# Two relational graph passes on one core: gathers grouped by three tiles in place of five, with a ring of sixteen groups

## What is computed

```python
def _rgcn_layer(x, src, dst, edge_type, w_rel, root, bias):
    seg = dst * NUM_REL + edge_type
    xs = x[src]
    sums = jax.ops.segment_sum(xs, seg, num_segments=N * NUM_REL)
    cnt = jax.ops.segment_sum(jnp.ones(seg.shape, x.dtype), seg, num_segments=N * NUM_REL)
    mean = (sums / jnp.maximum(cnt, 1.0)[:, None]).reshape(N, NUM_REL, -1)
    return jnp.einsum('nrd,rdo->no', mean, w_rel) + x @ root + bias
...
edge_type = jnp.argmax(msg[:, NODE_EMB_DIM:-NODE_EMB_DIM], axis=1)
h = relu(_rgcn_layer(layernorm_relu(x), ..., w_rel1, root1, b1))
x = x + _rgcn_layer(h, ..., w_rel2, root2, b2)
x = x + attention(layernorm_relu(x), edge_index, W_l, W_r, att, bias)
```

## Time and profile before

| what | us |
|---|---|
| median of 3 runs | 12271.99 (12270.22 to 12287.71) |
| span of the profiled execution | 12273.4 |
| prologue, to the first gather | 195.4 |
| pass 1, first gather to first gather of pass 2 | 195.4 to 4179.0 |
| pass 2, to the first gather of the attention pass | 4179.0 to 8166.8 |
| attention pass | 8166.8 to 12273.4 |

### The profile page before, as it was taken

How to read it: one execution, slowest core, us unless ns; L and a number is a source line. 1 busy time by engine, 2 the same in 40 slices (tenths; PEclk the granted TensorE clock), 3 DMA queues, 4 the chain that set the end, 5 groups by cost and what they waited for, 6 DMA issues and landing times. The chain is left out here.

```text
span 12273.4 us, 236908 instructions
## 1 busy us (share of the span) xinstructions
PE 8873.7 (72%) x59600; PEld 8089.9 (66%) x59600; DVE 7757.1 (63%) x17430; ACT 2044.9 (17%) x5895; POOL 8995.7 (73%) x9486
## 2 busy tenths in 40 slices
PE   2666677877777766666777777766777777777776
PEld 2566667777777666666777777755666666666666
DVE  4555456666666555545777777755666666766767
ACT  1000000000000000000000000014444444444442
POOL 2777777777777577777777777757777777777776
PEclk6778889999999888888988889888989998999888
DMA  5666445555555444444555555557888888888887
GB/s 132 138 138 138 86 94 116 116 117 116 117 117 117 91 82 82 82 81 95 117 116 117 116 117 117 117 122 203 236 237 233 235 235 235 236 234 235 237 235 207
DMA packets 1439046, 1838.34 MB, mean 150 GB/s; under 512 B 371751, under 2 KB 1003264, under 8 KB 1431525
## 3 DMA queue, kind: packets, MB, share of 16 engines
q0 software_dynamic: 300000, 634.20, 28.4%
q1 hardware_dynamic: 915809, 888.29, 26.5%
q10 hardware_dynamic: 221967, 300.69, 7.9%
HBM read 1361.75 MB, written 458.67 MB: 148 GB/s over the span
## 5 line engine op out<-in xcount | busy, mean ns | idle before, releaser
L653 POOL DMA_INDIRECT p_g<-htab,p_i x6250 | 5916.2, 947 | 1972.0 <-issue 1890.3
L883 PE MATMUL p_pg<-p_g,p_oh 128*120 x33600 | 4809.8, 307 | 1792.7 <-ACTq L679 1475.7
L883 PEld LDWEIGHTS p_pg<-p_g,p_oh 128*120 128x120 f32 x33600 | 4544.3, 212 | 2026.4 <-issue 1997.2
L1257 POOL DMA_INDIRECT a_g<-xlw,a_i x3125 | 2987.2, 956 | 1036.0 <-issue 869.0
L755 DVE SCALAR_TENSOR_TENSOR p_oh<-key,qbase,p_cols 128x600 f32<-128x600 f32 x3370 | 2803.1, 832 | 13.1 <-issue 13.1
L814 DVE SCALAR_TENSOR_TENSOR p_acc<-p_acc,cont,p_pg 120x129 f32<-120x129 f32 x3360 | 1166.8, 347 | 2580.0 <-PE p_pg L883 2338.4
L670 ACT ACTIVATE p_i<-src_i 128x5 int32<-128x5 int32 x1240 | 258.2, 208 | 7566.6 <-DMA p_g<-htab,p_i 6935.0
L1730 PE MATMUL a_px<-a_g,ident 128*128 x1450 | 736.8, 594 | 840.0 <-SPq L1312 782.5
L1719 PE MATMUL a_pg<-a_v,a_into 128*128 128x132 f32 x7000 | 968.6, 288 | 62.0 <-POOL a_v L1276 23.0
L1719 PEld LDWEIGHTS a_pg<-a_v,a_into 128*128 128x128 f32 x7000 | 902.5, 202 | 73.3 <-issue 31.3
L1730 PEld LDWEIGHTS a_px<-a_g,ident 128*128 128x128 f32 x1450 | 241.4, 209 | 921.4 <-issue 920.9
(11 more groups left out here) (231 smaller groups left out, 6831.3 us busy)
## 6 DMA issues: line engine op xcount, KB each, us to landing
a_xj<-xjw ACTq DMA_DIRECT2D x725, 330.0 KB
xjw<-a_g SPq DMA_DIRECT2D x625, 330.0 KB
partial<-p_acc SPq DMA_DIRECT2D x3360, 60.5 KB
a_dst<-in_dst_dram SPq DMA_DIRECT2D x625, 320.0 KB
p_s<-partial SPq DMA_DIRECT2D x2100, 60.5 KB
p_g<-htab,p_i POOLq DMA_INDIRECT x6250
a_g<-xlw,a_i POOLq DMA_INDIRECT x3125
a_xr<-xrw ACTq DMA_DIRECT2D x728, 66.0 KB
```

Source lines behind the costliest of these rows:

```text
L653: pool.indirect_dma_start(gath[:, (k * G + q) * W:(k * G + q + 1) * W], None, table, bass.IndirectOffsetOnAxis(ap=stage[k][:, q:q + 1], ax ...
L883: last = t.matmul(pg[bank(c, k)], onehot[b][:, q * KW:(q + 1) * KW], gath[:, ds(to + q * W, W1)], start=(q == 0), stop=(q == G - 1))
L1257: pool.indirect_dma_start(gbuf[k][:, q * W:(q + 1) * W], None, xlw, bass.IndirectOffsetOnAxis(ap=stage[k][:, q:q + 1], axis=0)).then_inc(s ...
```

## The change

In the two relational passes a group is three tiles (`RG`) in place of five: 1042 groups, the last one of two tiles, and 2100 steps of three products in place of 1680 of five (210 rounds in place of 168). The ring has 16 groups (48 tiles), slots go back nine groups later in place of five, and the node tiles are read from round 106 on in place of 64. The `match` instruction covers 360 columns in place of 600. The number of gathers, of windows and of node tiles stays, and so does the attention pass with its groups of five. In the prologue the rows of one number for each group grow from 625 to 1042 where they belong to the relational passes; the group's number in the packed table gets 11 bits; the last destinations of both kinds of group are loaded.

```diff
-QSTEPS = -(-(GROUPS + NW - 1) // UN) * UN
+RG = 3
+RGROUPS = -(-TILES // RG)
+QSTEPS = -(-(RGROUPS + NW - 1) // UN) * UN
...
-READ_AT = 64
+READ_AT = 106
...
-QSLOTS = 10
-FREED = 5
+QSLOTS = 16
+FREED = 9
...
-QPACK = 1024
-PTOP = (QSLOTS - 1) * G * W * QPACK + GROUPS
+QPACK = 2048
+RW = RG * W
+PTOP = (QSLOTS - 1) * RW * QPACK + RGROUPS
...
-                            sp.dma_start(last_i, dst.rearrange("(a g e) -> a g e", a=1, e=GE)[:, :, GE - 1]).then_inc(s_last, 16)
+                            ends = dst[0:(RGROUPS - 1) * RG * P].rearrange("(a g e) -> a g e", a=1, e=RG * P)
+                            sp.dma_start(last_i[:, 0:RGROUPS - 1], ends[:, :, RG * P - 1]).then_inc(s_last, 16)
+                            sp.dma_start(last_i[:, RGROUPS - 1:], dst[E - 1:E].rearrange("(a e) -> a e", a=1)).then_inc(s_last, 16)
+                            sp.dma_start(last_a, dst.rearrange("(a g e) -> a g e", a=1, e=GE)[:, :, GE - 1]).then_inc(s_last, 16)
...
-                        nc.gpsimd.iota(gnum, [[1, GROUPS]], base=0, channel_multiplier=0, allow_small_or_imprecise_dtypes=True).then_inc(s_iota, 1)
+                        nc.gpsimd.iota(gnum, [[1, RGROUPS]], base=0, channel_multiplier=0, allow_small_or_imprecise_dtypes=True).then_inc(s_iota, 1)
...
+                        nc.gpsimd.memset(key_f[:, TILES:], -1.0).then_inc(s_iota, 1)
...
-                            dve.wait_ge(s_last, 16)
+                            dve.wait_ge(s_last, 48)
...
-                                link(v.tensor_scalar(junk, psf[:, 0:GROUPS], snum[:, c:c + 1], 0.0, how, ALU.add, accum_out=to[:, c:c + 1]))
+                                link(v.tensor_scalar(junk[:, 0:of], psf[:, 0:of], snum[:, c:c + 1], 0.0, how, ALU.add, accum_out=to[:, c:c + 1]))
...
-                            for step in ring_steps(slots, GROUPS):
+                            for step in ring_steps(slots, RGROUPS):
...
-                                counted(1, gs, QCOLS, ALU.is_lt)
+                                counted(1, gs, QCOLS, ALU.is_lt, RGROUPS)
...
-                                counted(2, lw, WCOLS, ALU.is_le)
+                                counted(2, lw, WCOLS, ALU.is_le, RGROUPS)
...
-                                counted(3, gt, SCOLS, ALU.is_lt)
+                                counted(3, gt, SCOLS, ALU.is_lt, GROUPS)
...
-                            t.matmul(psf[:, 0:512], ones[0:1, :], of[0:1, 0:512], start=True, stop=True)
-                            t.matmul(psf[:, 512:GROUPS], ones[0:1, :], of[0:1, 512:GROUPS], start=True, stop=True).then_inc(s_psf, 1)
+                            for at in range(0, width, 512):
+                                upto = min(at + 512, width)
+                                last = t.matmul(psf[:, at:upto], ones[0:1, :], of[0:1, at:upto], start=True, stop=True)
...
-                        spread(0, finq)
-                        spread(1, lastw)
-                        spread(2, fint)
+                        spread(0, finq, RGROUPS)
+                        spread(1, lastw, RGROUPS)
+                        spread(2, fint, GROUPS)
...
-                gath = sbuf(st, f"{name}_g", [P, QSLOTS * G * W])
...
-                onehot = [sbuf(st, f"{name}_oh{k}", [P, G * KW]) for k in range(QLOOK)]
+                gath = sbuf(st, f"{name}_g", [P, QSLOTS * RW])
...
+                onehot = [sbuf(st, f"{name}_oh{k}", [P, RG * KW]) for k in range(QLOOK)]
...
-                            for q in range(G):
+                            for q in range(min(RG, TILES - RG * g)):
...
-                                    gath[:, (k * G + q) * W:(k * G + q + 1) * W], None, table,
+                                    gath[:, (k * RG + q) * W:(k * RG + q + 1) * W], None, table,
...
-                        for i in range(0, GROUPS // QSLOTS):
-                            for k in range(QSLOTS):
-                                group(QSLOTS * i + k, k)
-                        for k in range(GROUPS % QSLOTS):
-                            group(GROUPS - GROUPS % QSLOTS + k, k)
+                        for g in range(RGROUPS):
+                            group(g, g % QSLOTS)
...
-                                gate(act, "act", (s_g[k], 16 * G * (i + 1)))
+                                gate(act, "act", (s_g[k], 16 * (RG * i + min(RG, TILES - RG * (QSLOTS * i + k)))))
...
-                            v.scalar_tensor_tensor(onehot[k][:, :].rearrange("p (t n) -> p t n", t=G),
-                                                   key_f[:, ds(within(gp1 * G - G, TILES - G), G)].rearrange("p (t a) -> p t a", a=1).to_broadcast([P, G, KW]),
+                            v.scalar_tensor_tensor(onehot[k][:, :].rearrange("p (t n) -> p t n", t=RG),
+                                                   key_f[:, ds(within(gp1 * RG - RG, RGROUPS * RG - RG), RG)].rearrange("p (t a) -> p t a", a=1).to_broadcast([P, RG, KW]),
...
-                                                   colsp.rearrange("p (a n) -> p a n", a=1).to_broadcast([P, G, KW]),
+                                                   colsp.rearrange("p (a n) -> p a n", a=1).to_broadcast([P, RG, KW]),
...
-                                    gp1, to = count(packed[k]), within(packed[k] >> 10, (QSLOTS - 1) * G * W)
+                                    gp1, to = count_g(packed[k]), within(packed[k] >> 11, (QSLOTS - 1) * RW)
...
-                                    for q in range(G):
+                                    for q in range(RG):
...
-                                                        start=(q == 0), stop=(q == G - 1))
+                                                        start=(q == 0), stop=(q == RG - 1))
```

More of the change, by code:

```diff
@@ L152, in count_q, with count_g @@
     def count_q(value):
-        return value & 2047
+        return value & 4095
+    def count_g(value):
+        return value & (QPACK - 1)
     def within(value, top):
@@ L608, in rgcn_pass @@
             with ExitStack() as st:
-                gath = sbuf(st, f"{name}_g", [P, QSLOTS * G * W])
-                stage = [sbuf(st, f"{name}_i{k}", [P, G], I32) for k in range(QSLOTS)]
-                onehot = [sbuf(st, f"{name}_oh{k}", [P, G * KW]) for k in range(QLOOK)]
+                gath = sbuf(st, f"{name}_g", [P, QSLOTS * RW])
+                stage = [sbuf(st, f"{name}_i{k}", [P, RG], I32) for k in range(QSLOTS)]
+                onehot = [sbuf(st, f"{name}_oh{k}", [P, RG * KW]) for k in range(QLOOK)]
                 acc = [sbuf(st, f"{name}_acc{k}", [KW, W1]) for k in range(ALOOK)]
@@ L682, in _ @@
                         groups(0, QSLOTS, True)
-                        for i in range(1, GROUPS // QSLOTS):
+                        for i in range(1, RGROUPS // QSLOTS):
                             groups(i, QSLOTS, False)
-                        groups(GROUPS // QSLOTS, GROUPS % QSLOTS, False)
+                        groups(RGROUPS // QSLOTS, RGROUPS % QSLOTS, False)
                     @block.sync
@@ L815, in body @@
                                                            ALU.mult, ALU.add).then_inc(s_acc, 1)
-                                    match(s + QLOOK, b, count(groups[k]))
+                                    match(s + QLOOK, b, count_g(groups[k]))
                                 if chunk and 1 <= k <= 5:
@@ L830, in _ @@
                         for s in range(QLOOK):
-                            match(s, s, count(ahead[s]))
+                            match(s, s, count_g(ahead[s]))
                         all_rounds(dve, first, body)
```

49 lines of the change are left out of this document (25 added, 24 removed).

## The result

| | kernel before | changed kernel |
|---|---|---|
| median, us | 12,273.4 (12,270.2 to 12,287.7, 4 runs) | 12,685.4 (12,672.2 to 12,721.4, 4 runs) |
| ratio, 95% interval | | 1.0338 (1.0326 to 1.035): slower |
| profiled execution, span | 12,273.4 | 12,669.2 |
| mean granted clock of TensorE | 0.876 | 0.814 |

What follows compares the result with a forecast made beforehand. POOL's gathers were taken as the bound, with DVE taking over in pass 2's node-tile stage. 12,272 + 116 (that stage) + 24 (prologue) = 12,412 us; range for 8 in 10: 12,290 to 12,520.

Steps and rivals of the forecast that it cites:

- The bound before, the pace after: Both passes: POOL's gathers, 1.2485 us each, set the pace, 23.45 us a round before and 18.75 after.
- The match: DVE's match in each step: 832 ns at 600 columns falls to 585 ns at 360.
- The 18.1: Pass 2 node tiles: the skill's 435 ns match would bring DVE's floor to 18.1 us a round, under 18.75.
- The prologue: Before the first gather: longer rows and more single numbers to load add 24 us (20 to 49).
- VectorE's floor in pass 2: Pass 2 node-tile stage: DVE needs 19.9 us a round (19.6 to 20.1) against 18.75, costing 116 us.
- the ring only lends its lead: Ring of gathered tiles: it takes the first 26 us of lag but hands them back after the last gather.
- They cost nothing: Pass 1 node-tile stage and both passes' starts: PE (13.5 us a round) and DVE fit into 18.75, no cost.
- Pass 1 falls behind too: Rival, chance 0.10: pass 1's node-tile rounds take 19.3 us, adding 55 us, 12,467 in all.
- The bound of 20.5 a round and 177 us: Pass 2 node tiles: another 0.4 us a round of PE and DVE waits makes the floor 20.5, cost 177 us.
- After the last gathers: End of the passes: 19 steps in place of 16, each shorter, so no change (-5 to +3 us).
- Faster through the drains: Rival, chance 0.04: time after the last gathers shrinks by 50 us, 12,246 where POOL stays the bound.
- single numbers dear on SP: Rival, chance 0.05: loading the single numbers on SP makes the prologue cost 49 us, 12,437 in all.

Runs made afterwards that it cites:

- spread kernel: The changed kernel with each node tile's products spread over steps 0, 1 and 2 of its round: 12,376.1 us, ratio 1.008.
- short scaling: The spread kernel with VectorE scaling the sums of only two of the ten relations: 12,279.9 us, ratio 1.0004.
- the control: The kernel before (five tiles to a step) with its node products spread in the same way: 12,270.6 us, ratio 0.9997.

## Why the prediction was off, point by point

- *The bound before, the pace after*: right. Outside the node-tile stages POOL keeps 1.247 us a gather, and the waits that were added cost nothing.
- *The match*: 582 ns, forecast 585. The 18.1 that the prediction got for the floor from the Trainium skill ("VectorE: DVE Perf Modes", section on the TRN2 errata) came from setting the formula's 435 against the measured 832. The formula's own difference, 685 less 435, is 250 ns, as good as the 247 of the rows, and leaves the floor where the rows had it.
- *The prologue*: first gather at 220.8 us, 25.4 later, forecast 24 (its terms add up to 23.4).
- *VectorE's floor in pass 2*: right as a mechanism and over-sized. The undelayed round shown above takes 19.57 us, the lower bound, not 19.9, and those with the short block 19.70 on average: 0.95 us over the pace, 96 us over 101 rounds, where the sum had 116. The spread kernel has rounds of 19.46, and there the short scaling takes off 23.6 + 128.2 - 1.7 - 78.3 = 72 us. Most of it is not lost under way but stands after the last gather; that the ring only lends its lead was said and held.
- **"They cost nothing"**, of the node-tile stage of pass 1, is the step that failed, by 136.5 + 48.6 = 185 us. It took PE's 13.5 us a round from the busy time of the kernel before, measured at a clock of 0.92, and took the clock as given. With products removed it is 0.79, with as many added again as products of another kind 0.94, and at the low level the same round has 21 us of records, against a pace of 18.75. The rival "Pass 1 falls behind too" had the place, but 55 us and a chance of 0.10, and for want of this mechanism no better price.
- The same step failed in pass 2, where no term stood for it. The whole cost of pass 2 is 119.8 + 55.2 = 175 us. Above the 96 of the floor stand 51 rounds with the long block of node products, 1.56 us longer each, 80 us; together 176. That this part is the clock is read from the rounds of one kernel. The runs agree but do not part it from the place of the products: spreading them gave back 122.3 + 139.3 - 23.6 - 128.2 = 110 us of pass 2, and the clock rose with it. The bound of 20.5 a round and 177 us was in the text, as an addition that the shorter round could bring; the size came out so, the reason did not.
- *After the last gathers* no change was forecast; it was +48.6 and +55.2, which fits the ring's lag handed back, and goes with the two points above.
- *Faster through the drains, single numbers dear on SP*: neither came.

Prologue 25, pass 1 185, pass 2 175 and attention 10 make 395 of the profiled executions' 396.

## What to carry to other kernels

Before calling work on TensorE hidden, look at its granted clock in the stage, and count the records of a round at the low level too: taking work away from it can lower the clock and make what is left longer (here 0.92 to 0.79; the records of a round are 11 us at the high level and 21 at the low one). A loop with slack forgives where a lump of work stands (0.9997 in the control); once the pace is cut to the length of the round, spreading the same lump over three steps was worth 325 us. And the sign of a change of 1 to 3% can depend on the chip (3.4% slower here, 1.3% faster on chip 12): compare on more than one.

## What the runs showed of the hardware

- One product more in each step raised the granted clock of a stage from 0.79 to 0.94 and shortened the kernel by 1.1 points, though it does nothing.
- With the same instructions in another order the clock of that stage was 0.88.
- In a loop of steady work the clock can change from round to round: in pass 2 of the changed kernel blocks of 20 node-product records took 4.1 to 4.25 us and 2.44 us in turn, in rounds of 21.2 and 19.55 us.
- On two chips the kernel before takes 29 to 30% longer than on the others, at a clock of 0.78 in place of 0.88. In the changed kernel's profile on one of them TensorE's semaphore comes up to 10.5 us after VectorE is ready and the step's last product record has ended, and there the changed kernel is 1.3% faster than the kernel before in place of 3.4% slower.
